# First layer's FFN as three f16 products of high and low parts, with four GELU buffers

## The reference

```python
# first layer, cross-attention: keep the top 76 of 256 similarities in each row, gate with a sigmoid, mix with x
threshold = top_k(sim, 76)[0][:, :, -1:]
A = (sim >= threshold) * sigmoid(sim)          # made symmetric, then mixed with the normalised x
# first layer, FFN on xn = layernorm(x), 1024 hidden units in 16 blocks of 64
logits = xn @ Wr.T + br                        # 16 router logits for a token
mask   = the 4 blocks with the largest logits  # 64 hidden units each
h      = gelu(xn @ W1.T) * mask                # W1 is 1024 x 256
x      = x + tanh(g_ffn[0]) * (h @ W2.T)       # W2 is 256 x 1024
```

## Time and profile before

| what | us |
|---|---|
| median of 3 runs | 474.98 (474.36 to 478.52) |
| the profiled execution's own time | 475.87 |
| its span | 474.0 |
| the first layer's FFN on PE, first h unit to last result | 44.1 to 131.4 |
| mean granted TensorE clock | 0.971 |

### The profile page before, as it was taken

The page is one execution under the profiler, slowest core; times in us unless marked ns, Lnnn a source line. Parts: engine busy times, 40 slices in busy tenths (PEclk is TensorE's granted clock), DMA queues, the critical chain, the costliest instruction groups (busy, mean ns, idle before and its releaser), DMA issues. The chain is left out here.

```text
span 474.0 us, 8851 instructions
## 1 busy us (share of the span) xinstructions
PE 438.7 (93%) x2723; PEld 279.3 (59%) x2723; DVE 304.0 (64%) x886; ACT 252.0 (53%) x628; POOL 188.0 (40%) x190
## 2 busy tenths in 40 slices
PE   5886999899969999999999999999998899899987
PEld 2574877786734555555555555555566773644476
DVE  3989799955145766677676667757743748446612
ACT  3582445545314677667767766776666242045510
POOL 1650404041603566555465655546643005543000
PEclk9995999999977999999999999999999979999999
DMA  7643000000102343343334334212200799589202
GB/s 249 190 110 103 3 0 1 1 2 22 46 0 66 90 102 90 77 115 74 94 80 105 89 75 107 50 44 57 66 12 2 204 309 278 143 188 261 72 29 90
DMA packets 61448, 43.81 MB, mean 92 GB/s; under 512 B 22955, under 2 KB 54502, under 8 KB 61414
## 3 DMA queue, kind: packets, MB, share of 16 engines
q1 hardware_dynamic: 60646, 41.04, 32.6%
q0 software_dynamic: 768, 2.36, 2.5%
HBM read 27.25 MB, written 2.23 MB: 62 GB/s over the span
## 5 line engine op out<-in xcount | busy, mean ns | idle before, releaser
L1172 POOL TENSOR_TENSOR PB<-PB,inv 128x512 f32<-128x512 f32 x64 | 66.6, 1041 | 79.6 <-DVE inv L1222 79.4
L1111 ACT ACTIVATE PB<-ps,low 128x256 f32<-128x256 f32 x128 | 59.6, 471 | 31.0 <-DVE low L1216 31.0
L275 POOL TENSOR_TENSOR rot<-rot 128x512 f32<-128x512 f32 x48 | 61.1, 1273 | 32.6 <-DMA rot<-rot 32.6
L1216 DVE TENSOR_REDUCE low<-ps 128x2 f32<-128x512 f32 x64 | 44.1, 689 | 38.4 <-PE ps L1028 37.4
L255 DVE TENSOR_TENSOR rot<-ps,sinq 128x512 f32<-128x512 f32 x48 | 33.2, 692 | 16.6 <-PE ps L242 14.5
L1036 PE MATMUL ps<-ident,PB 128*128 128x128 f32 x256 | 41.1, 283 | 1.1 <-ACT PTS L1119 0.8
L1119 ACT ACTIVATE PTS<-ps 128x512 f32<-128x512 f32 x64 | 38.2, 597 | 7.2 <-PE ps L1036 5.1
L1036 PEld LDWEIGHTS ps<-ident,PB 128*128 128x128 f32 x256 | 27.7, 141 | 24.0 <-issue 19.9
L242 PE MATMUL ps<-XH,CH 128*128 128x512 f16 x96 | 37.6, 392 | 0.0
L242 PE MATMUL ps<-XL,CH 128*128 128x512 f16 x96 | 37.4, 390 | 0.0
L242 PE MATMUL ps<-XH,CL 128*128 128x512 f16 x96 | 37.4, 390 | 0.0
(11 more groups left out here) (246 smaller groups left out, 874.0 us busy)
## 6 DMA issues: line engine op xcount, KB each, us to landing
rot<-rot SPq DMA_DIRECT2D x64, 128.0 KB, 2.3
rot<-rot SPq DMA_DIRECT2D x64, 64.0 KB, 2.0
EGU<-in_L_ffn_W_gate_dram SPq DMA_DIRECT2D x8, 384.0 KB, 5.7
EGU<-in_L_ffn_W_up_dram SPq DMA_DIRECT2D x8, 384.0 KB, 5.8
ED<-in_L_ffn_W_down_dram SPq DMA_DIRECT2D x8, 384.0 KB, 6.6
rot<-in_L_ffn_W_dram SPq DMA_DIRECT2D x2, 1024.0 KB, 10.1
WQ<-in_L_xattn_Wq_dram SPq DMA_DIRECT2D x8, 256.0 KB, 3.0
WO<-in_L_xattn_Wo_dram SPq DMA_DIRECT2D x8, 256.0 KB, 3.1
```

The lines of the kernel that those rows point to most:

```text
L275: pool.tensor_tensor(g.RO[:, n, x, :], g.RO[:, n, x, :], g.TC[x][:, :], ALU.add).then_inc(g.sum_ok, 1)
L1111: e = act.activation(PB[t % 2][:, h, :], g.ps[:, SC + t % 2, h * S:(h + 1) * S], ACT.Exp, bias=low[:, t % 2, h:h + 1], scale=-1.0, accum_o ...
L1172: pool.tensor_tensor(PB[t % 2][:, :, :], PB[t % 2][:, :, :], inv[:, t % 2, :].unsqueeze(2).broadcast_to([P, 2, S]), ALU.mult).then_inc(nor ...
L1216: dve.tensor_reduce(low[:, t % 2, :], g.ps[:, SC + t % 2, :].rearrange("p (h s) -> p h s", h=2), AX.X, ALU.min).then_inc(low_ok, 1)
```

## The change

- The tiles that ACT fills with turned weights are now scaled by `UP` = 64 and are only the source of a split. POOL makes from each 512 columns a high part (cast to f16) and a low part (f32 minus high, in f16): `W1H`, `W1L`, `W2H`, `W2L` (`weight_parts`, eight times two instructions).
- The normalised, turned x gets a high part by a second ACT copy out of PSUM (`XTH`) and a low part on POOL (`turned_low`, once for a batch).
- Each f32 matmul against W1T becomes three f16 matmuls (high x high, low weight x high, high weight x low); each one against W2T likewise (`split`). PE's order is else as it was.
- `masked` now writes its product back to the GELU buffer in f32. ACT copies it to f16 (`hidden_high`), and POOL subtracts (`hidden_low`); for the last batch DVE does that subtraction. There are four GELU buffers, two of them in `rot`.
- GELU's scale is 1/64, and the FFN's gate is divided by 64 in a small added tile. GELU now waits for the low part four units back; the mask copy waits for the product two units back.
- `first(3)` on DVE now stands ahead of `rest(1)`. The norms use one semaphore less.

The core of the diff:

```diff
+                def turned_low(b):
+                    pool.wait_ge(xt_ok, 2 * b + 2)
+                    pool.tensor_tensor(XTL[:, :, :], XT[b % 2][:, :, :], XTH[:, :, :],
+                                       ALU.subtract).then_inc(xtl_ok, 1)
+                def weight_parts(first, k):
...
+                    pool.wait_ge(emptied, plain(n))
+                    pool.tensor_copy(hi, full).then_inc(wl_ok, 1)
+                    pool.wait_ge(wl_ok, 2 * (k if first else 4 + k) + 1)
+                    pool.tensor_tensor(lo, full, hi, ALU.subtract).then_inc(wl_ok, 1)
...
                 for b in range(B):
+                    if b >= 1:
+                        turned_low(b)
                     for n in range(UNITS):
                         masked(b, n)
+                        if b < B - 1 and n >= 1:
+                            hidden_low(b, n - 1)
                         if b == B - 1 and n >= 1:
                             add_partners(pool, g, 0, n - 1)
+                    if b < B - 1:
+                        hidden_low(b, UNITS - 1)
...
+                            for m, (hx, wx) in enumerate(split(HH[b % 2], HL[b % 2], W2H, W2L)):
+                                mm = pe.matmul(g.ps[:, YB, D * j:D * j + D], hx[:, o, j * P:(j + 1) * P],
+                                               wx[:, o, :], start=(o == 0 and j == 0 and m == 0),
...
+                        for m, (wx, xx) in enumerate(((W1H, XTH), (W1L, XTH), (W1H, XTL))):
+                            if n == 0 and m == 2:
+                                pe.wait_ge(xtl_ok, b + 1)
...
+                def hidden_high(b, n):
+                    act.wait_ge(hf_ok, UNITS * b + n + 1)
...
                 def mask(b, n):
                     u = UNITS * b + n
                     act.wait_ge(mask_ps, u + 1)
+                    if u >= 2:
+                        act.wait_ge(hf_ok, u - 1)
...
                         if n >= 1:
                             mask(b, n - 1)
+                        if n >= 2:
+                            hidden_high(b, n - 2)
                         if n == UNITS - 1:
                             mask(b, n)
+                            hidden_high(b, n - 1)
+                            hidden_high(b, n)
...
+                first(B - 1)
                 rest(B - 3)
-                first(B - 1)
...
+                hidden_low(0)
                 rest(B - 2)
                 rotate_query(dve, g, 0, 2, QA)
+                for n in range(1, UNITS):
+                    hidden_low(n)
                 second(B - 1)
```

More of the change, by code:

```diff
@@ L336, in stage_first_layer @@
         br = sb("br", [P, NBLK])
-        W1T = sb("W1T", [P, KT, HID])
-        W2T = sb("W2T", [P, HID // P, D])
+        W1T = g.rot[:, 8:12, :].rearrange("p (k a) s -> p k (a s)", k=KT)
+        W2T = turned[:, :, :].rearrange("p a (o d) -> p (a o) d", d=D)
+        W1H, W1L = [sb(f"W1{part}", [P, KT, HID], F16) for part in "HL"]
+        W2H, W2L = [sb(f"W2{part}", [P, HID // P, D], F16) for part in "HL"]
         WrT = sb("WrT", [P, KT, NBLK])
@@ L345, in stage_first_layer @@
         XT = [spare[:, 2 * u:2 * u + 2, :] for u in range(2)]
+        XTH, XTL = [spare[:, 6 + u, :].bitcast(F16).rearrange("p (k s) -> p k s", k=KT) for u in range(2)]
+        ffn_gate = sb("ffn_gate", [P, 1])
         FS = sb("FS", [P, 2 * DQ])
@@ L476, in masked, with hidden_low @@
                     pool.wait_ge(ms_ok, u + 1)
[L477 to L480, removed]
+                    pool.tensor_tensor(GL[u % 4][:, :, :], GL[u % 4][:, :, :], MS[u % 2][:, :, :],
+                                       ALU.mult).then_inc(hf_ok, 1)
+                def hidden_low(b, n):
+                    pool.wait_ge(hh_ok, UNITS * b + n + 1)
+                    low_part(pool, b, n)
+                def turned_low(b):
[3 more added lines that the diff above has]
+                def weight_parts(first, k):
+                    flat = lambda x: x[:, :, :].rearrange("p a b -> p (a b)")[:, 512 * k:512 * k + 512]
+                    hi, lo, full = [flat(x) for x in ((W1H, W1L, W1T) if first else (W2H, W2L, W2T))]
+                    n = (N_W1 if first else N_W2) + k
+                    pool.wait_ge(emptied, plain(n))
+                    pool.tensor_copy(hi, full).then_inc(wl_ok, 1)
+                    pool.wait_ge(wl_ok, 2 * (k if first else 4 + k) + 1)
+                    pool.tensor_tensor(lo, full, hi, ALU.subtract).then_inc(wl_ok, 1)
                 def fold_second(k):
@@ L721, in _ @@
                         act.activation(W1T[:, k, 512 * h:512 * h + 512], bank(N_W1 + 2 * k + h),
-                                       ACT.Copy).then_inc(emptied, 1)
+                                       ACT.Copy, scale=UP).then_inc(emptied, 1)
                 for q in range(4):
-                    act.activation(W2T[:, 2 * q:2 * q + 2, :], bank(N_W2 + q), ACT.Copy).then_inc(emptied, 1)
+                    act.activation(W2T[:, 2 * q:2 * q + 2, :], bank(N_W2 + q), ACT.Copy, scale=UP
+                                   ).then_inc(emptied, 1)
                 o = bank(N_WR)
@@ L776, in _ @@
                     act.activation(XT[b % 2][:, :, :], g.ps[:, TB, :], ACT.Copy).then_inc(xt_ok, 1)
+                    act.activation(XTH[:, :, :], g.ps[:, TB, :], ACT.Copy).then_inc(xt_ok, 1)
                     for n in range(UNITS):
@@ L826, in second @@
                     dve.wait_ge(y_ps, b + 1)
+                    dve.wait_ge(gam_ok, 4)
                     for j in range(2):
@@ L833, in second, with hidden_low @@
                     norm_stats(dve, g, n2, b)
+                def hidden_low(n):
+                    dve.wait_ge(hh_ok, UNITS * (B - 1) + n + 1)
+                    low_part(dve, B - 1, n)
                 def rest(b):
```

82 lines of the change are left out of this document (54 added, 28 removed).

## The result

The changed kernel takes 485.89 us (median of 4 runs, 483.45 to 487.4), the kernel before 474.74 beside it: 1.0212 times as long, 95% interval 1.0176 to 1.0248. The forecast was 477.6, its range ended at 482.5; the time lies 3.4 us above the range. The profiled execution took 486.87, its span is 485.1 (before 475.87 and 474.0), at a mean granted TensorE clock of 0.954 (before 0.971).

What follows compares the result with a forecast made beforehand. DVE's top-k rounds were taken to bound the first half, a chain over four engines the last batch. 0 + 3.0 - 2.2 + 1.9 = +2.7 on 475.87, against the median 477.6 us; range 473.0 to 482.5.

Steps and rivals of the forecast that it cites:

- DVE's chain: DVE from `first(1)` to the end of `A(3)`, 40.75 us before: two to three more POOL collisions and a wait, +3.0.
- `A(3)` to `norm_turn(3)`: PE's stretch after DVE's chain: cheaper result units make it 7.95 us instead of 10.19, -2.2.
- the last batch: `norm_turn(3)` to the context products, 23.75 us before: PE saves 2.4, gives back 1.6, serial chain adds 2.7; +1.9.
- the low clock: PE slowing after idle time: through two units in the last batch it costs 2.6 us; priced in rival 2.
- rival 2: Slower by over 1%: DVE held twice in each pair, +4 on `A(3)`, 481.6 us, or PE at low clock; chance 0.15.
- The wait for `norm_root(1)`: In DVE's chain: ACT's `norm_root(1)` stands behind `hidden_high(0, 3)` and comes 0.4 us after DVE asks.
- The chain in series: Last batch after the fourth h unit: two passes over the engines, 4.3 and 5.4, 9.7 us instead of 7.02, +2.7.
- the wait for the low part: Last batch: `result(3, 0)` waits on mask copy, product, `hidden_high` and DVE's `hidden_low`, giving back 1.6 us.
- `first(1)`, 0 forecast: Start of DVE's chain after the weights' split: stays at 56.7, +0, between -0.5 and +1.5 us.
- the second pass of the last chain: Last batch: from the last mask through copy, product, `hidden_high`, POOL wait and subtraction to the last result, 5.4 us.
- 1 (hardly any collision): DVE's chain: POOL's instructions fall between DVE's steps, about 474.5 us, at best 472; chance 0.20.
- 3 (PE was the bound): Whole kernel: PE's savings show as they are, up to 15 us less, 461 to 470 us; chance 0.05.

Runs made afterwards that it cites:

- the kernel with POOL held back: Only x against W1T in three f16 products; in batches 1 and 2 POOL's first product waits for the next batch's `A`: 471.2 us, 0.9902 of the kernel before.
- the kernel with the filler: Changed kernel plus useless matmuls in PE's idle times, ahead of `symmetric(2)`, `symmetric(3)`, `result(3, 1)` and `result(3, 2)`: 484.81 us, 1.0214 of the kernel before.
- the first half alone: Changed kernel with only x against W1T in three f16 products, h and W2T in f32: 478.95 us, 1.0084 of the kernel before.
- the kernels that have it by construction: POOL's first product in batches 1 and 2 waits for the next batch's `A`: 471.2 us with only x against W1T in f16, 481.14 on the changed kernel.
- the same wait on the kernel before: Kernel before, where in batches 1 and 2 POOL's first product waits for `A` of the next batch: 478.56 us, ratio 1.0042.
- last mask first: Changed kernel with `mask(3, 3)` ahead of `result(3, 1)` on PE instead of behind it: 481.48 us, 1.0139 of the kernel before.

## Why the prediction was wrong

The forecast had +2.7 for 11.1 us. Of the 8.4 that it lacks, 2.0 lie in DVE's chain, 1.8 from `A(3)` to `norm_turn(3)`, 3.2 in the last batch, 0.7 ahead of the chain and 0.7 behind the context products. Two steps failed: the count of held instructions, and the low clock, which the sum put at nothing and which makes about 3 us of the lack.

**DVE's chain: the wrong count.** The sum said "between two and three more collisions, 2.6 us" and took one held instruction of each pair, as the rows of before have it. Of what was after, both were held wherever POOL worked without a gap: +5.0. I had put this case down as rival 2 and gave it 0.15 together with the clock. The working looked at POOL's number of instructions (nine for four); the runs show that the gap between products decides. Five instructions a batch cost as much (a chain of 45.4) as nine, and the four buffers remove the gap, which the prediction priced at nothing. The rule of the Trainium skill ("SBUF — State Buffer", section "SBUF: two separate sides"), an exclusive lock for a whole instruction, is what the rows of the changed kernel follow, and in size too: of the 2.35 the first 0.92 are what was left of the product of 72.72, and the pair ends at 75.42, 0.16 after the product of 73.95. The rows beside copies follow it as well.

**The wait for `norm_root(1)`, +0.4:** it did not appear; DVE's busy time is 45.14 of 45.70.

**A(3) to `norm_turn(3)`, -2.2 forecast, -0.4 measured.** The result units had the forecast 1.3 us or nearly (5.44 for four). What was missing is the clock: PE idled 3.27 us for the late `A(3)`, and `symmetric(3)` took 3.4 us at a granted 0.55, where the kernel with POOL held back has 2.0. The prediction named such idle time, but priced it in rival 2, not in the sum.

**The last batch, +1.9 forecast, +5.1 measured.** The chain in series was right, the held subtraction too: the working had 0.8 of waiting for POOL and 0.55, and 1.40 came. Up to the end of the fourth hidden unit the change gained 0.2 us, not 0.8; the wait for the low part was 1.39, about as forecast (1.6), but PE's own saving was 2.0 instead of 2.4, and the wait for the norm's XN grew from 0.41 to 0.83. From there (129.46) the context products came 12.3 us later, where the forecast was 9.7. By the kernel with the filler some 1.5 of these 2.6 are the low clock after PE's waits of 2.79 and 2.65 us, for which the sum had nothing and the bounds of this part +4. The fourth subtraction took 1.52, where 1.15 was counted. The rest, some 0.7, I can't place.

**`first(1)`, 0 forecast, +0.7.** `turned_low(0)` ended at 47.69, forecast 47.8. In the kernels with both halves `first(1)` starts between 57.2 and 58.5, in those with the first half alone between 55.3 and 56.5, in those without the change between 56.65 and 57.6; where the program up to it is the same, it still varies by over 1 us. This size is not explained, nor is the 0.7 behind the context products.

**Sums.** By its own terms the forecast is 477.7, the second pass of the last chain 5.5 and POOL's nine instructions 10.9 us; that changes nothing.

**Rivals.** 1 (hardly any collision) did not come; the kernels that have it by construction reach a chain of 39.4 to 40.5. 2 came in its mechanism, both instructions held and a low clock behind it, but the time is 4.3 us above its 481.6 too. 3 (PE was the bound) did not come either, and the savings on PE show only where DVE's chain is free: the first half with POOL held back is 4.5 us faster than before, while the same wait on the kernel before costs 2.5. Of the 4.6 us that its profiled span is shorter, 2.4 lie in the three pieces of the forecast, 1.3 in the earlier `first(1)` and 0.9 behind the context products; the last two I can't put down to the change.

Open: why the changed kernel's runs spread over 4 us. Where POOL's products fall against DVE's pairs followed PE's clock some us before in the profiles of two runs (last mask first, filler), but I have no run that sets it.

## What to carry to other kernels

Before POOL gets work, list DVE's instructions that it can hold and see whether POOL pauses there; a buffer more can take that pause away, and the time lost is then counted as DVE's own busy time (14.7 us more here, of which 5.7 are the four new subtractions). Where POOL's results aren't needed at once, let it wait for the end of DVE's sensitive pair, with buffers enough that the engines ahead of it go on. In a chain in series, look for two steps released by the same event on the two engines: they collide every time, not by chance.

## What was new about the hardware

- A held instruction of DVE ended at a fixed time after the one of POOL: `norm_apply` 0.15 us, `A` 0.28, `var` 0.03, the f16 low part 0.55. POOL's copies f32 to f16 with one input held `norm_apply` like products and subtractions (0.67 and 0.69 for 0.41). A `var` that began with 0.15 us of a product left lost nothing.
- The hold goes both ways: POOL's additions beside DVE's low parts took 1.71 or 1.72 instead of 1.27, the products after a held DVE instruction 1.31 to 1.44.
- DVE's x plus attention, which reads PSUM and one SBUF tile, took its own 0.88 at 57.40 beside a product of POOL (56.89 to 58.16), and MAX8 pairs stayed at 0.74 in the changed kernel's chain, whatever POOL did.
